# A four-layer graph network on one core: GpSimd's gather loops written out, with indices read from whole arrays

## The reference

```python
x = x + L0(h)  # two graph convolutions, degree-normed, 64 -> 128 -> 64
x = x + L1(h)  # relu(((1 + eps) * h + segment_sum(relu(h[src] + edge_attr), dst)) @ W.T + b)
x = x + L2(h)  # K = 8 rounds: softmax attention over incoming edges, h = segment_sum(h[src] * a, dst)
x = x + L3(h)  # K = 10 rounds: h = segment_sum((h * src_norm)[src], dst) * dst_norm, mixed with fixed weights
```

## Time and profile before

| what | us |
|---|---|
| median of 3 runs (8538.08 to 8546.38) | 8542.38 |
| span of the profiled execution | 8552.4 |
| POOL busy | 5712.2 (67%) |
| DVE busy | 5422.9 (63%) |
| PE busy | 1658.7 (19%) |
| ACT busy | 822.9 (10%) |

### The profile page before, as it was taken

How to read it: one execution, slowest core, us unless ns; L and a number is a source line. 1 busy time by engine, 2 the same in 40 slices (tenths; PEclk the granted TensorE clock), 3 DMA queues, 4 the chain that set the end, 5 groups by cost and what they waited for, 6 DMA issues and landing times.

```text
span 8552.4 us, 64167 instructions
## 1 busy us (share of the span) xinstructions
PE 1658.7 (19%) x7784; PEld 1201.8 (14%) x7784; DVE 5422.9 (63%) x18625; ACT 822.9 (10%) x2010; POOL 5712.2 (67%) x5754
## 2 busy tenths in 40 slices
PE   5744434310355135500022102000000000000000
PEld 2233323210244023300022102000000000000000
DVE  6778868658888634367788788656556664444520
ACT  0011111100122431100000000000006000000000
POOL 6777767656777767667677572666640767777777
PEclk8755555555555555555555555555555555555555
DMA  7034424210355433934444213243322222433310
GB/s 255 0 90 95 98 66 101 61 32 10 73 130 129 100 93 93 297 83 109 122 110 109 61 45 83 44 41 44 42 31 84 47 58 47 41 42 39 37 24 19
DMA packets 1197893, 660.37 MB, mean 77 GB/s; under 512 B 1057324, under 2 KB 1070561, under 8 KB 1195205
## 3 DMA queue, kind: packets, MB, share of 16 engines
q10 hardware_dynamic: 880608, 373.78, 16.0%
q0 software_dynamic: 174720, 155.54, 13.0%
q1 hardware_dynamic: 142436, 129.95, 5.1%
HBM read 236.69 MB, written 425.58 MB: 77 GB/s over the span
## 4 chain that ended last, share of the span: by engine, by line
POOL 37%; DVE 28%; issue 21%; DMA 7%; ACT 3%; POOLq 1%; PE 1%; DVEq 1%; ACTq 1%; SPq 0%
POOL G L575 16%; POOL look L575 7%; DVE G L2173 5%; POOL pair L575 5%; POOL seatmap L579 5%; POOL out L579 4%; DVE st L1637 2%; ACT wide_block L1179 2%; DVE G L2163 1%; DMA G<-tab,idxs 1%; DVE xm L1654 1%; POOL wide_block L575 1%; DVE wide_block L1658 1%; DVE xm L1667 1%; DVE G L2485 1%
## 5 line engine op out<-in xcount | busy, mean ns | idle before, releaser
L575 POOL DMA_INDIRECT G<-tab,idxs x1260 | 1317.7, 1046 | 453.9 <-issue 358.4
L575 POOL DMA_INDIRECT look<-flagtab,idxs x588 | 628.6, 1069 | 206.6 <-issue 170.2
L575 POOL DMA_INDIRECT G<-alt_e,idxs x420 | 441.3, 1051 | 151.0 <-issue 120.3
L575 POOL DMA_INDIRECT pair<-lookup,idxs x392 | 423.6, 1081 | 141.0 <-issue 116.8
L575 POOL DMA_INDIRECT X<-in_x,dst_gat x392 | 421.4, 1075 | 124.4 <-issue 124.4
L579 POOL DMA_INDIRECT seatmap<-vals,idxs x392 | 405.1, 1034 | 140.7 <-issue 116.6
L575 POOL DMA_INDIRECT G<-alt_d,idxs x392 | 403.7, 1030 | 138.9 <-issue 115.2
L1328 PE MATMUL TR<-w4T,shared 128*128 128x64 f32 x2356 | 465.3, 388 | 157.3 <-ACT shared L1043 157.3
L1637 DVE BATCH_NORM_STATS2 st<-xin 128x6 f32<-128x64 f32 x3136 | 419.3, 212 | 112.6 <-issue 63.8
L1328 PEld LDWEIGHTS TR<-w4T,shared 128*128 128x128 f32 x2356 | 451.9, 298 | 249.5 <-issue 249.5
L1345 PE MATMUL HP<-ident,tcar 128*64 128x128 f32 (+1 forms) x21 | 8.6, 409 | 2329.3 <-DVEq L1562 2318.6
(11 more groups left out here) (528 smaller groups left out, 7614.6 us busy)
## 6 DMA issues: line engine op xcount, KB each, us to landing
tab<-wide_block ACTq DMA_DIRECT2D x294, 448.0 KB, 3.8
tab<-rowsB ACTq DMA_DIRECT2D x98, 448.0 KB, 3.8
xin<-tab SPq DMA_DIRECT2D x84, 448.0 KB
raw<-G ACTq DMA_DIRECT2D x84, 448.0 KB
xin<-in_x SPq DMA_DIRECT2D x56, 448.0 KB, 5.1
tab<-wide_block ACTq DMA_DIRECT2D x2, 12544.0 KB, 55.5
out<-shared ACTq DMA_DIRECT2D x56, 448.0 KB, 5.6
staged<-wide_block SPq DMA_DIRECT2D x20, 1120.0 KB, 5.6
```

The costliest lines, as they stand in the source:

```text
L575: pool.indirect_dma_start(to, None, table, bass.IndirectOffsetOnAxis(ap=index, axis=0), bounds_check=bound, oob_is_err=False).then_inc(s, 16)
```

## The change

The loops over chunks of the seat scatter, the lookup, the edge rows and the four sweeps become Python loops, so that every chunk has instructions of its own. The indices are taken straight from the whole arrays (`end0`, `src0`, `eidx`, `idxA`), the scattered places from `place0`, and looked-up pairs land in `found`. The copies into `idxs` and `vals`, the copies out of `pair`, and the waits for them go; waits against registers become waits against constants, except for `used` and `raw_stored` in the sweeps. The limits on DMAs under way (a chunk starts when the chunk two before it has landed) stay. `vals` and `pair` go from the on-chip memory. The flag lookups, `narrow_sweep` and `refill` are as before.

```diff
-            def seat(c, s):
-                pool.tensor_copy(idxs[:, s, :], cols(end0, c))
-                pool.tensor_copy(vals[:, s, :], cols(place0, c)).then_inc(pool_step, 1)
-                pool.wait_ge(pool_step, r_step.more(1))
-                ...
-                    scatter(seatmap, idxs[:, s, j:j + 1], vals[:, s, j:j + 1], seated[s])
+            for c in range(NCH):
+                if c >= 2:
+                    pool.wait_ge(seated[c % 2], 16 * CH * (c // 2))
+                for j in range(c * CH, c * CH + CH):
+                    scatter(seatmap, end0[:, j:j + 1], place0[:, j:j + 1], seated[c % 2])
...
-            def find(c, s):
-                pool.tensor_copy(idxs[:, s, :], cols(src0, c)).then_inc(pool_step, 1)
-                ...
-                    gather(pair[:, s, j, :], lookup, idxs[:, s, j:j + 1], found_some[s])
-            def keep(c, s):
-                pool.wait_ge(found_some[s], r_fs2[s].more(16 * CH))
-                pool.tensor_copy(found[:, ds(c * CH, CH), :], pair[:, s, :, :]).then_inc(pool_step, 1)
-                ...
+            for c in range(NCH):
+                if c >= 2:
+                    pool.wait_ge(found_some[c % 2], 16 * CH * (c // 2))
+                for j in range(c * CH, c * CH + CH):
+                    gather(found[:, j, :], lookup, src0[:, j:j + 1], found_some[c % 2])
...
-            def attr_rows(c, first):
-                pool.tensor_copy(idxs[:, 0, :], cols(eidx, c)).then_inc(pool_step, 1)
+            def attr_rows(c):
                 last_row(edge_attr)
                 for h in (0, 1):
-                    if not first:
-                        pool.wait_ge(attr_stored[h], r_as[h].more(16))
+                    if c:
+                        pool.wait_ge(attr_stored[h], 16 * c)
                     for j in range(h * half, h * half + half):
-                        gather(G[:, 1, j, 0:D], edge_attr, idxs[:, 0, j:j + 1], attr_gathered[h])
+                        gather(G[:, 1, j, 0:D], edge_attr, eidx[:, c * CH + j:c * CH + j + 1], attr_gathered[h])
...
-                with pool.Fori(0, SPLIT // 2) as i:
-                    for s in (0, 1):
-                        ...
-                        pool.tensor_copy(idxs[:, s, :], cols(idxA, 2 * i + s)).then_inc(pool_step, 1)
-                        pool.wait_ge(pool_step, r_step.more(1))
+                last_row(tab)
+                for c in range(SPLIT):
+                    s = c % 2
+                    pool.wait_ge(used[s], r_used[s].reg)
+                    pool.sem_inc(pool_waited, 1)
+                    r_used[s].skip(1)
+                    pool.wait_ge(raw_stored[s], r_raw[s].reg)
+                    pool.sem_inc(pool_waited, 1)
+                    r_raw[s].skip(16)
+                    for j in range(CH):
+                        to = gathered_rest if k == "d" and s == 1 and j >= HALF_CH else gathered[s]
+                        gather(G[:, s, j, 0:D], tab, idxA[:, c * CH + j:c * CH + j + 1], to)
+                if k == "c":
+                    last_row(edge_attr)
+                    for c in range(SPLIT, NCH):
+                        s = c % 2
                         pool.wait_ge(used[s], r_used[s].reg)
                         pool.sem_inc(pool_waited, 1)
                         r_used[s].skip(1)
                         for j in range(CH):
+                            gather(ea[:, s, j, :], edge_attr, eidx[:, c * CH + j:c * CH + j + 1], edges_late[s])
```

More of the change, by code:

```diff
@@ L143, in _build @@
         look = sb("look", [P, 2, CH])
-        vals = sb("vals", [P, 2, CH])
-        pair = sb("pair", [P, 2, CH, 2])
         xin = sb("xin", [P, 2, CH, D])
@@ L559, in _ @@
             r_lk = [Reached(pool, f"pool_lk{s}") for s in (0, 1)]
-            r_seat = [Reached(pool, f"pool_seat{s}") for s in (0, 1)]
-            r_fs2 = [Reached(pool, f"pool_found{s}") for s in (0, 1)]
             r_fg = Reached(pool, "pool_fg")
@@ L606, in _ @@
             last_row(seatmap)
-            def seat(c, s):
-                pool.tensor_copy(idxs[:, s, :], cols(end0, c))
-                pool.tensor_copy(vals[:, s, :], cols(place0, c)).then_inc(pool_step, 1)
-                pool.wait_ge(pool_step, r_step.more(1))
-                pool.sem_inc(pool_waited, 1)
-                last_row(seatmap)
-                for j in range(CH):
-                    scatter(seatmap, idxs[:, s, j:j + 1], vals[:, s, j:j + 1], seated[s])
-            def seat_landed(s):
-                pool.wait_ge(seated[s], r_seat[s].more(16 * CH))
-                pool.sem_inc(pool_waited, 1)
-            for s in (0, 1):
-                seat(s, s)
-            with pool.Fori(1, NCH // 2) as i:
-                for s in (0, 1):
[L625 to L628, removed]
+            for c in range(NCH):
[3 more added lines that the diff above has]
+                    scatter(seatmap, end0[:, j:j + 1], place0[:, j:j + 1], seated[c % 2])
+            for s in (0, 1):
+                pool.wait_ge(seated[s], 16 * CH * (NCH // 2))
             pool.dma_start(smap[0:NHI, :], seatmap.rearrange("(p j) f -> p (j f)", p=NHI)).then_inc(map_loaded, 16)
@@ L639, in _ @@
             last_row(lookup)
-            def find(c, s):
-                pool.tensor_copy(idxs[:, s, :], cols(src0, c)).then_inc(pool_step, 1)
-                pool.wait_ge(pool_step, r_step.more(1))
-                pool.sem_inc(pool_waited, 1)
-                last_row(lookup)
-                for j in range(CH):
-                    gather(pair[:, s, j, :], lookup, idxs[:, s, j:j + 1], found_some[s])
-            def keep(c, s):
-                pool.wait_ge(found_some[s], r_fs2[s].more(16 * CH))
-                pool.sem_inc(pool_waited, 1)
-                pool.tensor_copy(found[:, ds(c * CH, CH), :], pair[:, s, :, :]).then_inc(pool_step, 1)
-                pool.wait_ge(pool_step, r_step.more(1))
-                pool.sem_inc(pool_waited, 1)
-            for s in (0, 1):
[L657 to L663, removed]
+            for c in range(NCH):
[3 more added lines that the diff above has]
+                    gather(found[:, j, :], lookup, src0[:, j:j + 1], found_some[c % 2])
+            for s in (0, 1):
+                pool.wait_ge(found_some[s], 16 * CH * (NCH // 2))
             pool.sem_inc(found_all, 1)
@@ L751, in _ @@
             gather(X[:, FC, :], x, fidx[:, F_DST:F_DST + 1], x_front)
-            with pool.Fori(HEAD, MID) as c:
-                attr_rows(c, False)
+            for c in range(HEAD, MID):
+                attr_rows(c)
             for k in KINDS:
@@ L760, in _, with edge_rows @@
             pool.wait_ge(seats_cleared, 64)
[L761 to L769, removed]
+            def edge_rows(c, s):
                 last_row(edge_attr)
                 for j in range(CH):
-                    gather(edge_slot[s][:, j, :], edge_attr, idxs[:, s, j:j + 1], edges_gathered[s])
-            edge_rows(MID, 0, True)
+                    gather(edge_slot[s][:, j, :], edge_attr, eidx[:, c * CH + j:c * CH + j + 1], edges_gathered[s])
+            edge_rows(MID, 0)
             for h in (0, 1):
                 pool.wait_ge(attr_stored[h], 16 * MID)
-            edge_rows(MID + 1, 1, True)
+            edge_rows(MID + 1, 1)
             for s in (0, 1):
```

37 lines of the change are left out of this document (5 added, 32 removed).

## The result

| | before | after |
|---|---|---|
| median, us | 8540.23 (4 runs, 8532.88 to 8546.38) | 8456.78 (4 runs, 8454.03 to 8462.99) |
| ratio, 95% interval | | 0.9907 [0.9893, 0.9921] |
| span of the profiled execution | 8552.4 | 8461.3 |

The change is worth 83 us (80 when it was timed again as e11); 84 were predicted (8458). The sum is right, but its terms are not: seats and lookup gave more than 43.3 us, sweeps a and b less than 14.4 each, and the unchanged code behind sweep d, for which the sum had nothing, gave some 12 us.

A forecast was written before the change was run, and what follows sets the result against it. POOL and DVE were taken to share the bound, stage by stage. Terms 43.3 + 0 + 14.4 + 14.4 + 1.9 + 10 = 84.0 us gave 8458 us; the forecast's own range was 8446 to 8474.

The forecast's parts named there:

- Seats, 31.6 us of POOL: Seat scatter: removing 28 pairs of copies and their waits, less 28 plain gaps, shortens POOL by 31.6 us.
- The term per boundary: Chunk boundaries written out: copy and wait go, one plain gap of 0.30 us stays; 0.78 us a chunk taken in sweeps.
- Lookup, 40.9: Lookup: removing copies in and out and their waits, less plain gaps, shortens POOL by 40.9 us.
- 43.3 us paid for both: At found_all: POOL is 72.5 us earlier, but only DVE's wait of 43.3 us is paid; POOL then idles 29.2.
- Edge rows, 0: Ten edge-row chunks: 8 us less on POOL, paid with nothing, as POOL idles 28.82 us for front rows behind them.
- Sweeps a and b, 14.4 each: Sweeps a and b: POOL holds them, so 17 x 0.78 + 1.1 = 14.4 us is gained in each.
- Sweep c, 1.9: Sweep c: DVE-bound, only its first two waits shorten, 1.1 + 0.8 = 1.9 us; bounds 0 and 23.7.
- Sweep d, 10: Sweep d: gain limited by DVE's idle time and raw stores that stop POOL; 10 us, between 4 and 11.3.
- Rival 1: Written-out POOL code stops for instruction fetch, 7.1 us each, in seats, lookup and sweeps: slower, 8578 us; chance 5%.
- Rival 2: Sweeps do not pay: a buffer wait replaces the copy in a, b and d; 8494 us; chance 12%.
- Rival 4: No effect: gathers are paced by their queue, so the gap returns elsewhere; 8542 us; chance 3%.
- Rival 3: DVE gets faster without POOL's copies: lookup 18, seats 5, sweeps 13, 36 us in all; 8422 us; chance 6%.

The follow-up runs named there:

- e11: The changed kernel itself, timed again beside later runs: 8463.43 us, ratio 0.9909 to the kernel before.
- e3: Kernel before with only the edge rows (ten chunks) written out: 8548.63 us, ratio 1.0003.
- e4: Kernel before with the four sweeps written out, each chunk still copying its indices into idxs and waiting for the copy: 8542.71 us, ratio 0.9996.
- e8: Kernel before with DVE's first loop of ten dense pairs written out: 8550.26 us, ratio 1.0005.
- e2: Kernel before with only the four sweeps written out, without index copies: 8525.71 us, ratio 0.9971 to before.
- e1: Kernel before with only seat scatter and lookup written out, edge rows and sweeps still looped: 8484.06 us, ratio 0.9925.
- e9: e7 with an eleventh dense pair ahead of the found_all wait and one fewer behind order_ready: 8435.65 us, ratio 0.9875 to before.
- e5: Changed kernel plus four useless DVE operations ahead of the addition in sweep a's first 18 chunks: 8460.51 us, ratio 0.9899 to before.
- e12: Changed kernel with the addition in sweep a's first 18 chunks replaced by an equally long one-input operation: 8459.97 us, ratio 0.9905 to before.
- e10: e9 plus four small useless DVE operations ahead of the addition in the first 18 chunks of sweeps a and b: 8419.89 us, ratio 0.9858 to before.
- e7: Changed kernel with DVE's first loop of ten dense pairs written out as well: 8461.23 us, ratio 0.9898 to before.

## Why the prediction was right, and where not

The table has the gain by stretch, from the mean of three traces of kernels that take the time of before (before, e3, e4) to the mean of two traces of the changed kernel (after, e11). From sweep a on a stretch starts at the first gather of a sweep.

| stretch | predicted, us | by the traces, us |
|---|---|---|
| to DVE passing `found_all` | 43.3 | 48.4 |
| from there to sweep a | 0 | 2.4 |
| sweep a, to sweep b | 14.4 | 10.1 |
| sweep b, to sweep c | 14.4 | 3.9 |
| sweep c, to sweep d | 1.9 | 0.8 |
| sweep d, to its last gather | 10 | 9.3 |
| behind it | 0 | 12.5 |
| all | 84.0 | 87.3 (83 by the times) |

The second stretch takes 1850.0 us in after and 1844.0 in e11, which are the same kernel, so its 2.4 us tell nothing.

- *Seats, 31.6 us of POOL:* 24. The term per boundary held (gaps of 0.33), but three stops at every 112th DMA took 6.0, 1.7 and 3.7 us instead of about 2.2 each: 5 of the 7 us. It was hidden. *Lookup, 40.9:* 38.5.
- *43.3 us paid for both:* the mechanism is right: DVE's wait is gone, POOL idles there, and the writing out of DVE's loop in the old kernel (e8) gains nothing. The size is off. The wait is 47 us in three traces more, and where seats and lookup are written out, and DVE's loop is as it was, DVE arrives at 1157.4 to 1160.3 us (six traces). In before, e2, e3 and e4 it would have come at 1162.3 to 1162.9, the end of its last dense operation plus 0.66. So 49 to 52 us are paid at `found_all` by the six traces against that of e3 (1208.89). One trace of before was read as exact. e1's trace is 68 us shorter than the mean of the three: 50.2 to `found_all`, 8.4 from there to sweep a, 1.2 in the sweeps and 8.3 behind sweep d; that is where its 62.6 us lie.
- *Edge rows, 0:* 0 (e3). The cover was 28.82 us, and e9 shows the point where it ends.
- *Sweeps a and b, 14.4 each:* about 10 and 4. This is the step that failed. It took the gathers' duration as a property of the gather. It is also one of the phase: each 0.8 us taken from POOL's boundary moved its gathers against DVE's addition, from just beside it to inside it. a: 14.4 - 4.4 = 10.0, measured 351.0 - 340.6 = 10.4; b: 14.4 - 9.5 = 4.9, measured 4.3. The hold itself costs more than 4.4 and 9.5, as the shorter DMAs give some 2 us back in each sweep. In e2, which doesn't have them, the gathers are 7.1 and 11.0 us longer than in e3 and e4 (263.1 and 269.1 us in all against 256.0 and 258.1, means of the two), and the sweeps gain 7.1 and 2.3. e5 and e12 show the cause in a. In b it is shown less directly: the same ending of 0.87 us behind the addition (L2220, 26 gathers) and behind the product L1604, and e10, which moves it.
- *Sweep c, 1.9:* about 1, DVE-bound as read. Its gathers rose from 1076 to 1130 ns, without a price. *Sweep d, 10:* 9.6 from the front rows fetched at c's end (4796.18 us before, 4731.99 after) to those at d's (5347.21 and 5273.41), DVE's waits used up.
- *Behind sweep d, no term:* 12.5. The sum took the unchanged code as unchanged in time. Its indirect DMAs are shorter (above), for a reason that stays open.
- *Rival 1, instruction fetch:* not at the size that it needed. Stops in straight code of POOL come by count as those in the loops do, and e4 is equal to the loop. But the first of them in the seats took 5.5 to 6.1 us in all nine kernels with the seats written out, and 2.2 in the five others. *Rival 2:* no raw store stops POOL in a or b for over 3 us in all; in d the stores do, for 16.1, as the forecast had allowed. *Rival 4:* no.
- *Rival 3, DVE faster:* not in the sweeps. DVE's arrival 2 to 5 us earlier is in its direction and a quarter of its 18 + 5 us at most. e7 and e8 come near to isolating it: DVE's code is the same, with and without POOL's copies beside it, and its last dense operation ends at 1101.06 and 1101.77 us, 0.7 apart.

The misses, some +5 at `found_all` and +12 behind sweep d against -15 in sweeps a and b, cancelled. That the total came out within 1 us was luck.

The Trainium skill's lock ("SBUF — State Buffer", section "SBUF: two separate sides") names a DVE operation with two SBUF inputs against a GpSimd operation that reads SBUF. I weighed it only for DVE as the side that is held. These traces agree with it for the other side where the gather comes second, as in the 194 cases of the last section. That it is the reading of the index column in SBUF which is held is the Trainium skill's rule applied; no run here put the column elsewhere.

## What to carry to other kernels

Two engines that keep step repeat the same collision in every turn, so a cut on one of them has to be checked against what its later instructions now start beside: read the durations by position in the turn, not the mean. A wait on the other engine caps what a cut can pay, and it should be read from several executions where it carries half the sum. Once the wait is paid, look at where the slack has gone, as it may let work move (here a dense pair, 28 us more than the change gave). The stretches that an edit doesn't touch have to be compared too, or what they gain is put down to the edit's own terms.

## What the runs showed of the hardware

- An indirect DMA that begins inside an operation of DVE with two SBUF inputs ends 0.87 us behind that operation's end. In the trace after this holds (within 0.04) for all 194 gathers and scatters that began inside L1604 with over 0.3 us of it left (median 1.31 us, up to 1.72; none began less than 0.2 us into it), for 20 at L2175 and 26 at L2220. It is not so beside an operation with one of its two inputs in PSUM, or with one input at all: 53 at L1681 took 1.00 us by the median and 1.09 at most, 32 beside the reductions of L1616 took 1.00. Nor does it always hold at the very start: of 13 that began inside L1613 the six at 0.02 to 0.04 us into it took 1.00 us, the seven from 0.06 on were held. A case of the one-PSUM kind and one of a held gather:

```profile
629.02 1.09 DVE L1681 TENSOR_TENSOR agg<-TR,b1b 128x896 f32<-128x896 f32 x1 [0.79 <-PE TR L1284]
629.46 1.00 POOL L571 DMA_INDIRECT X<-lookup,X  x1 [0.30 <-issue]
```

```profile
3032.91 1.09 DVE L2175 TENSOR_TENSOR agg<-G,xin 128x896 f32<-128x896 f32 x1
3033.09 1.78 POOL L571 DMA_INDIRECT G<-tab,idxA  x1 [0.31 <-issue]
```

  Beside L1600, whose inputs both lie in SBUF too, only 57 of 170 were held. Why is open.
- DVE's loop of ten pairs stopped 7 us at each of nine turns; written out it did not (e7, e8), though its code is the longer for it. The Trainium skill ("Runtime: NRT & Kernel Launch", section "Instruction fetch mechanics") says that a taken branch outside the window of prefetched code forces a fetch; the stops at the turns agree. Later copies of the same loop had none in the traces before and after, which no run here explains.
- The same indirect DMA has a plain duration that differs a little from kernel to kernel: 972 to 974 ns for a scatter into `out` in nine kernels, 982 to 984 in five. With 5303 of them, 7 ns each (the flag lookups' difference) would be some 37 us of POOL's work, an estimate.
